# Two reorderings on TensorE in a graph-transformer kernel: row tiles turned a feature group sooner, and a feed-forward chunk's first product ahead of the last chunk's second ones

## What is computed

```python
for l in range(L):                      # L = 2
    ...
    agg = jax.ops.segment_sum(w[:, :, None] * v[srcidx], tgt, num_segments=n)
    attn = agg.reshape(n, D) @ Wo[l].T + bo[l]
    x = _batchnorm(x + attn, g1[l], beta1[l])
    ff = jax.nn.relu(x @ W1[l].T + b1[l]) @ W2[l].T + b2[l]
    x = _batchnorm(x + ff, g2[l], beta2[l])
```

## Time and profile before

| | us |
|---|---|
| runs, three | 3894.41, 3896.67, 3905.98 |
| median | 3896.67 |
| span of the profiled execution | 3095.6 |
| output projection, layer 0 / layer 1, TensorE's first to last matmul | 1371.3 to 1465 / 2497.5 to 2591 |
| feed-forward, layer 0 / layer 1, the same | 1469.8 to 1523 / 2595.5 to 2649 |

### The profile page before, as it was taken

One profiled execution on the slowest core, in us unless ns is written; L12 is line 12 of the kernel. 1 busy time (PEld: TensorE's weight loads), 2 busy tenths in 40 slices (PEclk: granted clock), 3 DMA queues, 4 the chain that ended last, 5 costly groups with the idle time before them and its releaser, 6 DMA issues.

```text
span 3095.6 us, 78344 instructions
## 1 busy us (share of the span) xinstructions
PE 2657.9 (86%) x32605; PEld 2143.5 (69%) x32605; DVE 1629.2 (53%) x3272; ACT 1321.1 (43%) x3690; POOL 1115.8 (36%) x1130
## 2 busy tenths in 40 slices
PE   5999997999999999758899788888888678599998
PEld 4877885777777777546488577777777465477777
DVE  5236785555555555456512355555554645656553
ACT  3324443555555555422232255555555322333432
POOL 0000002666666666400001267777777111222110
PEclk8999998999999999979999899999999889799998
DMA  5642003988899998641024489999999431122211
GB/s 195 228 175 107 31 28 140 317 313 316 309 331 322 317 325 297 222 121 41 14 97 154 160 321 354 352 349 347 350 347 352 126 113 57 38 89 92 69 59 58
DMA packets 231795, 621.75 MB, mean 201 GB/s; under 512 B 39008, under 2 KB 45792, under 8 KB 231427
## 3 DMA queue, kind: packets, MB, share of 16 engines
q0 software_dynamic: 137088, 466.78, 42.2%
q1 hardware_dynamic: 94339, 149.78, 14.6%
HBM read 538.80 MB, written 103.39 MB: 207 GB/s over the span
## 4 chain that ended last, share of the span: by engine, by line
PE 60%; DMA 16%; DVE 8%; POOL 7%; issue 6%; ACT 2%; SPq 0%; DVEq 0%; POOLq 0%; ACTq 0%
PE ps L1179 6%; DMA Y<-KVd,srcE 5%; PE ps L574 5%; PE ps L575 4%; PE ps L576 4%; DMA aggd<-stage,segs 4%; PE ps L1222 4%; PE ps L1209 4%; PE ps L774 3%; POOL Y L1096 3%; PE ps L942 2%; PE ps L944 2%; PE ps L943 2%; PE ps L1186 2%; PE ps L1872 2%
## 5 line engine op out<-in xcount | busy, mean ns | idle before, releaser
L1096 POOL DMA_INDIRECT Y<-KVd,srcE x449 | 430.2, 958 | 230.6 <-issue 115.8
L1370 ACT ACTIVATE stage<-ps,stage 128x128 f32<-128x128 f32 x832 | 294.8, 366 | 115.3 <-PE ps L1186 112.4
L1096 POOL DMA_INDIRECT WA<-KVd,srcE x186 | 179.3, 964 | 361.8 <-PE ps L576 268.1
L1351 ACT ACTIVATE work<-ps 128x512 f32<-128x512 f32 x309 | 179.8, 597 | 303.8 <-PE ps L1179 303.5
L1179 PE MATMUL ps<-ident,Y 128*128 128x128 f32 x1796 | 252.2, 280 | 32.2 <-DMA Y<-KVd,srcE 26.8
L1351 ACT ACTIVATE G<-ps 128x512 f32<-128x512 f32 x315 | 181.8, 597 | 223.5 <-PE ps L1179 223.1
L1277 DVE COPY G<-ps 128x512 f32<-128x512 f32 x208 | 143.8, 691 | 245.8 <-PE ps L1186 243.0
L574 PE MATMUL ps<-Wh,xs 128*128 128x512 f32 x600 | 238.7, 398 | 31.2 <-DVE xs L514 31.2
L1179 PEld LDWEIGHTS ps<-ident,Y 128*128 128x128 f32 x1796 | 199.2, 143 | 70.5 <-issue 49.3
L575 PE MATMUL ps<-Wl,xs 128*128 128x512 f32 x600 | 236.9, 395 | 0.0
L576 PE MATMUL ps<-Wh,xs 128*128 128x512 f32 x600 | 236.5, 394 | 0.0
(11 more groups left out here) (383 smaller groups left out, 6775.2 us busy)
## 6 DMA issues: line engine op xcount, KB each, us to landing
KVd<-stage SPq DMA_DIRECT2D x96, 256.0 KB, 2.0
aggd<-work SPq DMA_DIRECT2D x6, 2048.0 KB, 7.4
Qd<-stage SPq DMA_DIRECT2D x48, 256.0 KB, 2.0
G<-aggd SPq DMA_DIRECT2D x48, 256.0 KB, 2.7
Y<-KVd,srcE POOLq DMA_INDIRECT x449
Y<-in_x SPq DMA_DIRECT2D x4, 1536.0 KB, 14.7
G<-mixq SPq DMA_DIRECT2D x24, 256.0 KB
mixd<-rowsb SPq DMA_DIRECT2D x24, 256.0 KB
```

Of the source, the lines that this page charges most:

```text
L1096: pool.indirect_dma_start(out=kvs[a], out_offset=None, in_=KVd[l][:, :], in_offset=bass.IndirectOffsetOnAxis(ap=srcE[:, n:n + 1], axis=0)) ...
L1351: act.activation(kT[n % len(kT)], banks(l)[place_of(l, "k", n) % len(banks(l))][:, :], ACT.Copy).then_inc(out_a, 1)
L1370: last = act.activation(pT[g % len(pT)][:, P * i:P * (i + 1)], SC[g % 2][:, P * i:P * (i + 1)], ACT.Exp, bias=smin[:, t:t + 1], scale=-1.0 ...
```

## The change

In the output projection a new helper says which row tiles of chunk c+1 are turned behind product f of chunk c: two behind f = 0, one behind f = 1, one behind f = 2, none behind f = 3. VectorE's low parts move in the same way.

In the feed-forward stage the first product gets a function of its own, `inner`. TensorE does first product 0 ahead of the loop, and in round c first product c+1 and then the four second products of chunk c. First products now have banks 4 and 5 in turn, and second product f has bank f. VectorE's and ScalarE's programs keep their order there; only the banks that they read are others.

```diff
+        def turned_behind(c, f):
+            rows = NODE_TILES[c + 1] if c + 1 < NCK else []
+            return (rows[0:2], rows[2:3], rows[3:4], [])[f]
...
-                    if c + 1 < NCK and f < len(NODE_TILES[c + 1]):
-                        turn_row(NODE_TILES[c + 1][f])
+                    for t in turned_behind(c, f):
+                        turn_row(t)
+
+            def inner(c):
+                c0, cn = CHUNKS[c]
+                if c >= 2:
+                    pe.wait_ge(relu, NCK * l + c - 1)
+                is_normal(pe, 2 * l, c)
+                for k in range(4):
+                    mm = pe.matmul(PS[4 + c % 2][:, 0:cn], W1[:, k, :], xT[:, k, c0:c0 + cn], start=(k == 0), stop=(k == 3))
+                mm.then_inc(w1_mm, 1)
+
+            inner(0)
             for c, (c0, cn) in enumerate(CHUNKS):
-                for i in range(5):
-                    e = 5 * c + i
-                    bank, o = PS[e % 4], e - 4
...
+                if c + 1 < NCK:
+                    inner(c + 1)
+                pe.wait_ge(relu, NCK * l + c + 1)
+                for f in range(4):
+                    if c:
+                        pe.wait_ge(ff_add, WO * l + 4 * (c - 1) + f + 1)
                     else:
-                        pe.wait_ge(ff_add, WO * l + 4 * (o // 5) + o % 5)
...
+                        pe.wait_ge(wo_add, WO * l + WO - 3 + f)
+                    pe.matmul(PS[f][:, 0:cn], W2[:, f * P:(f + 1) * P], work[:, c % 3, 0:cn], start=True, stop=True
+                              ).then_inc(w2_mm, 1)
...
-                act.activation(work[:, c % 3, 0:cn], PS[5 * c % 4][:, 0:cn], ACT.Relu, bias=vec[:, C_B1 + l:C_B1 + l + 1]
+                act.activation(work[:, c % 3, 0:cn], PS[4 + c % 2][:, 0:cn], ACT.Relu, bias=vec[:, C_B1 + l:C_B1 + l + 1]
...
-                    if c + 1 < NCK and f < len(NODE_TILES[c + 1]):
-                        low_row(NODE_TILES[c + 1][f])
+                    for t in turned_behind(c, f):
+                        low_row(t)
...
-                    dve.scalar_tensor_tensor(out=xT[:, f, c0:c0 + cn], in0=PS[(5 * c + f + 1) % 4][:, 0:cn],
+                    dve.scalar_tensor_tensor(out=xT[:, f, c0:c0 + cn], in0=PS[f][:, 0:cn],
```

## The result

The changed kernel takes 3934.16 us (median of 20 runs) against 3890.49 for the kernel before (20 runs). The two medians lie 43.7 us apart. The ratio is 1.0077, with a 95% interval from 1.0048 to 1.0105, so it is slower by 30 us (19 to 41); it leaves out the changed kernel's five slowest runs, 3947.94 us and above. The forecast was 36.0 us slower, at 3932.7.

What follows compares the result with a forecast made beforehand. TensorE carries 60% of the chain, so its waits for low parts and the ReLU were judged. -17.3 + 0.2 + 31.3 + 21.8 = +36.0 us made span 3095.6 into 3131.6; with 801.1 outside, 3932.7, range 3908 to 3945.

Steps and rivals of the forecast that it cites:

- The projection: Output projection: ten TensorE waits of 1.73 us for VectorE's low parts at chunk starts go, gaining 17.3 us.
- The wait for tile 6: Output projection: tile 6, turned a group sooner, waits once for its fetch behind three weight loads, 0.2 us.
- The gaps: Feed-forward: first products wait for VectorE's scaling in ten gaps of about 4.2 us, costing 31.3 us in both layers.
- The clock: Feed-forward: TensorE's granted clock falls behind the new gaps, costing 21.8 us, with bounds of 0 and 27.
- The rule of the Trainium skill: Feed-forward: a TensorE that waits every round begins each at half the clock; by it +36.0 us, without it +14.2.
- Rival (a): Feed-forward: the clock stays at 1.00 in the gaps; +14.2 us, 3910.9, slower by 0.36%; chance 0.13.
- Rival (b): Feed-forward: the scaling doesn't hold first product c+1, so the kernel is faster by 23.6 us, 3873; chance 0.05.
- Rival (c): Output projection: no gain, each chunk's start still waits 1.73 us for a later low part or row; 3950; chance 0.06.
- (d): Feed-forward: something between, with gaps shorter than the rows say; within 0.3%; chance 0.06.
- The time outside the span: Whole kernel: 3896.67 - 3095.6 = 801.1 us taken to lie outside the profile's span and to stay as it is.

Runs made afterwards that it cites:

- fill16: Changed kernel with 16 unused matmuls in each feed-forward gap, ahead of the wait for the scaling; 3907.81 us, ratio 1.0044 to the kernel before.
- scale_sooner: Changed kernel with VectorE's scaling moved one chunk sooner (chunk c+2 in round c); 3862.85 us, ratio 0.9928 to the kernel before.
- fill8: Changed kernel with 8 unused matmuls in each feed-forward gap; one time, 3944.74 us, beside 3906.52 for the kernel before on that chip.

## Why the prediction was right

- **The projection.** Ten waits of 1.73 us were to go, one of 0.2 to come: -17.1. Measured -16.9, and that it is so near is luck: errors of both signs cancel. In layer 1, where nothing comes in the way, the stage gained 10.0 us and not 5 x 1.73 = 8.65: the period of a chunk, from TensorE's start to its next in the timelines, fell from 14.8 to 12.8 us, so by 2.0. From start to start, the turn behind group 3 and the wait took 2.32 us; now the second turn behind group 0 adds 0.44 (two turns take 0.79, one takes 0.35), and the matmuls of groups 3 and 0, which follow each other unbroken, take 0.1 less. Layer 0 gave 7.0 only, for two reasons. The wait for tile 6 was 1.4 us in place of 0.2: TensorE came to the tile 8.3 us behind its first matmul, as forecast, but the fetch landed at 9.6 and not at 8.5. The estimate had taken one trace's landing as fixed. The other reason had no term in the sum. From the first matmul of chunk 6 (53 columns) to the first scaling, the changed kernel took 10.8 us, and the kernel before 9.1 and 8.7 in its two traces; the clock fell while TensorE worked on this chunk without a gap. The same 49 matmuls in the changed kernel, and then in fill16, where the same code took 8.7; TensorE is busy with them for 7.47 and 5.41 us:

```profile
1853.50:1861.00 7.50, 7.47 (x49) 0.70 0.01 2
```

```profile
1868.10:1875.60 7.50, 5.41 (x49) 0.85 0.01 2
```

- **The gaps.** The step that carried the sign was that VectorE's unchanged order puts the scaling of chunk c+1 behind the adds of chunk c-1. The gap was put at 4.20 and is 4.09. The price of the gaps alone, 31.3, is 31.4 in fill16. In the parts of a round, a first product behind a wait takes 3.51 start to start in fill16 (1906.86 to 1910.37), as estimated; from there to VectorE's first add it is 1.06 and not 1.14, and the path from the scaling to TensorE is 0.10 and not 0.05.
- **The clock.** 21.8 us were taken from two gaps elsewhere in the trace, one at 1.6 and one at 2.9 us. Measured 22.3. All eight gaps of 4.09 us brought the clock down. Most full rounds of 13.7 us are 11.19 plus 2.5; the first of layer 0 lost 1.7, the second 2.6, and the two rounds with the short last product lost 1.8 each, where 1.7 was put. That a fall would come had more support than the earlier trace rows show, since other gaps of that trace, down to 2.8 us, were followed by a lower clock:

```profile
2986.10:2988.90 2.80, 0.00 (x0) 1.00 0.04 14
2988.90:2995.90 7.00, 6.97 (x32) 0.76 0.00 0
```

The size put in was the mean of two unlike rows, between bounds of 0 and 27 us; that it came within a microsecond of the measured one is luck.

- **The rule of the Trainium skill** (TensorE: Matmul & The Clock Gate, HAM oscillation — how this bites in real kernels), that a loop which waits in each round begins each at half the clock, agrees with the trace of the changed kernel, with one exception: in layer 0's first such round the clock was 1.00 for the first 1.15 us of the product and 0.50 behind that. Rival (a), in which the clock stays, fell: fill16 is what it would have looked like, at 1.0044.
- **Rival (b)** had put the gain at 23.6 us if the scaling did not hold the product. scale_sooner is that case: the projection -9.9 - 9.8, the feed-forward -4.1 - 4.7, together -28.5, and 27.2 us by the medians. The sum had it some 4 to 5 us too small: a chunk of the projection gives 2.0 us and not 1.73, a round of the feed-forward takes 6.87 us and not 7.02, which were two products of 3.51, and the adds of chunk 4 take 5.53 and not 6.04, since the last scaling no longer stands in between.
- **Rival (c)** fell: the waits for low parts are at 2 x 1.41. So did **(d)**.
- **The time outside the span** was a wrong reading. It did no harm, since the sum took differences of two stages only, which are alike in both profiles; had a term been taken as a share of the span, it would have rested on a span a fifth too short.

By the stages the change costs 36.8 us, by the ratio 30 (19 to 41), by the two medians 43.7. The 20 runs of the two kernels spread over 48 and 75 us, so the times bear out the sign and not the last ten microseconds, and that 3934.16 lies 1.5 us from the forecast time is in part luck. The stages tell it more sharply: 53.7 us lost in the feed-forward, where the forecast had 31.3 + 21.8 = 53.1, and 16.9 gained in the projection, where it had 17.1.

## What to carry to other kernels

When one engine's work is moved ahead, look for the other engine's instruction that feeds it, and move that by as many rounds; here one call in VectorE's loop decided between 0.77% slower and 0.7% faster. Count the order of both engines round by round before trusting that a wait is hidden: removing a wait of 0.87 us made one of 4.09. And price an idle TensorE with the clock that it costs behind it, 2.5 us of 5.7 a round here. Where such a gap can't be avoided, matmuls whose results nobody reads can be cheaper than idle time: 16 a gap saved 22 us here.

## What the runs showed of the hardware

- Behind a TensorE gap of 4.09 us the clock fell in every one of eight rounds, and cost 1.7 to 2.6 us. Behind gaps of 2.2 us it fell in four of eight (fill8), behind those of 1.73 us at the chunks' starts in none of the ten in the kernel before. Filled with matmuls whose results nobody reads, until 0.4 us of idle time were left, it did not fall.
- The clock also fell with no gap at all, in the 53-column chunk that ends the projection (granted clock 0.70 over 7.5 us in the changed kernel, TensorE busy for 7.47 of them), and how early differs between traces of one code: from the chunk's first matmul to the first scaling it was 8.7 us in fill16 and 10.8 in the changed kernel.
- One profile of a kernel can have a span 800 us shorter than another of the same kernel, with as many instructions, so a single profile's span is to be held against the usual time before shares are read from it.
- The landing of one 256 KB fetch behind three loads of 1 MB took 10.5, 11.7 and 13.5 us from its issue in three traces with the same transfers, two of them of the same kernel.
